# First self-attention of a two-layer decoder: the causal mask of the maximum's scores, added by VectorE in PSUM in place of two TensorE products

## What is computed

```python
q3 = (x @ wq).reshape(b, t, h, 3).transpose(0, 2, 1, 3)
k3 = (x @ wk).reshape(b, t, h, 3).transpose(0, 2, 1, 3)
v = (x @ wv).reshape(b, t, h, hd).transpose(0, 2, 1, 3)
dot_scores = jnp.einsum('bhtd,bhsd->bhts', q3, k3) * scale
geo_bias = q_on_dir[..., :, None] * k_on_dir[..., None, :]
scores = jnp.where(causal, dot_scores + geo_bias, -jnp.inf)
attn = jax.nn.softmax(scores, axis=-1)
out = jnp.einsum('bhts,bhsd->bhtd', attn, v)
```

## Time and profile before

| | us |
|---|---|
| median of 3 runs | 1267.47 |
| lowest and highest | 1267.25, 1268.99 |
| the profiled execution, its own time | 1272.5 |
| span of that execution, first to last instruction | 1270.6 |
| TensorE matmul busy over the span | 1150.3 (91%) |
| VectorE busy | 719.7 (57%) |
| ScalarE busy | 565.0 (44%) |
| GpSimd busy | 105.4 (8%) |
| mean granted TensorE clock | 0.956 of full speed |

### The profile page before, as it was taken

The page is one execution under the profiler, slowest core; times in us unless marked ns, Lnnn a source line. Parts: engine busy times, 40 slices in busy tenths (PEclk is TensorE's granted clock), DMA queues, the critical chain, the costliest instruction groups (busy, mean ns, idle before and its releaser), DMA issues.

```text
span 1270.6 us, 19991 instructions
## 1 busy us (share of the span) xinstructions
PE 1150.3 (91%) x7418; PEld 720.2 (57%) x7418; DVE 719.7 (57%) x1054; ACT 565.0 (44%) x1084; POOL 105.4 (8%) x147
## 2 busy tenths in 40 slices
PE   4999999898988988869988999999999999998797
PEld 2453443442222322247866777877787887786465
DVE  4344445667888789661426466465646666673213
ACT  1344344154545555751214566456635564562210
POOL 0112232112100000010001000010001000100100
PEclk7799899898979999979999999999999999999799
DMA  7012212320000000000023233123634964400000
GB/s 205 14 51 100 89 37 100 115 76 1 1 1 1 1 1 1 1 18 1 1 67 112 62 91 74 34 52 83 150 85 100 214 144 101 101 18 1 1 17 17
DMA packets 56962, 74.20 MB, mean 58 GB/s; under 512 B 12443, under 2 KB 33446, under 8 KB 56870
## 3 DMA queue, kind: packets, MB, share of 16 engines
q1 hardware_dynamic: 53110, 69.26, 21.4%
q10 hardware_dynamic: 3760, 3.67, 0.9%
HBM read 36.20 MB, written 15.73 MB: 41 GB/s over the span
## 4 chain that ended last, share of the span: by engine, by line
PE 79%; DVE 9%; issue 5%; ACT 4%; DMA 1%; POOL 1%; SPq 1%; ACTq 0%; POOLq 0%; DVEq 0%
PE p_unit L1665 20%; PE p_ring L1665 12%; PE p_out L1789 9%; PE p_ring L1685 8%; PE p_ring L1766 8%; PE p_ring L1732 7%; PE p_out L1755 6%; DVE halves L1454 2%; PE p_unit L1857 2%; PE p_ring L1710 1%; ACT prob_b L1238 1%; DVE prob_a L1468 1%; DVE x L1560 1%; PE p_ring L1724 1%; PE p_ring L1703 1%
## 5 line engine op out<-in xcount | busy, mean ns | idle before, releaser
L1454 DVE TENSOR_REDUCE halves<-p_ring 128x2 f32<-128x1024 f32 x128 | 156.2, 1220 | 65.8 <-PE p_ring L1710 65.6
L1252 ACT ACTIVATE prob_a<-p_ring 128x1024 f32<-128x1024 f32 x128 | 130.6, 1022 | 101.6 <-PE p_ring L1732 101.4
L1434 DVE TENSOR_REDUCE nmax<-p_ring 128x2 f32<-128x1024 f32 (+1 forms) x128 | 156.0, 1219 | 33.7 <-PE p_ring L1685 33.6
L1270 ACT ACTIVATE probT_b<-p_ring 128x512 f32<-128x512 f32 x144 | 84.5, 598 | 202.2 <-PE p_ring L1766 200.7
L1238 ACT ACTIVATE prob_b<-p_ring,nmax 128x512 f32<-128x512 f32 (+1 forms) x192 | 158.6, 837 | 18.3 <-DVE nmax L1434 18.0
L1685 PE MATMUL p_ring<-stacks 128*128 128x512 f32 x512 | 151.4, 418 | 8.9 <-ACT prob_b L1238 5.3
L1487 DVE COPY probT_b<-p_ring 128x512 f32<-128x512 f32 x112 | 77.1, 688 | 133.5 <-PE p_ring L1766 133.0
L1766 PE MATMUL p_ring<-ident,prob_b 128*128 128x128 f32 x1024 | 134.5, 274 | 0.3 <-ACT probT_b L1270 0.3
L1766 PEld LDWEIGHTS p_ring<-ident,prob_b 128*128 128x128 f32 x1024 | 116.2, 141 | 23.5 <-issue 14.8
L1732 PE MATMUL p_ring<-x_q,x_kq 32*128 32x512 f32 x512 | 124.4, 658 | 2.9 <-DVE halves L1454 2.9
L1454 DVE TENSOR_REDUCE wide_max<-p_ring 128x2 f32<-128x256 f32 (+3 forms) x64 | 52.6, 823 | 90.3 <-PE p_ring L1703 90.3
(11 more groups left out here) (226 smaller groups left out, 1614.1 us busy)
## 6 DMA issues: line engine op xcount, KB each, us to landing
stacks<-x_kd SPq DMA_DIRECT2D x64, 256.0 KB, 5.9
stacks<-splitH_b SPq DMA_DIRECT2D x80, 128.0 KB, 2.3
stacks<-splitL_b SPq DMA_DIRECT2D x80, 128.0 KB, 2.4
x_kd<-early SPq DMA_DIRECT2D x19, 256.0 KB, 2.0
x_v<-x_vd SPq DMA_DIRECT2D x8, 512.0 KB, 4.1
x_kd<-xT SPq DMA_DIRECT2D x13, 256.0 KB, 2.0
x_vd<-early SPq DMA_DIRECT2D x11, 256.0 KB, 2.0
a_st<-a_image SPq DMA_DIRECT2D x64, 32.0 KB, 1.8
```

The source lines that it names most:

```text
L1252: nc.scalar.activation(prob_place(key), slot_of("S2", key), ACT.Exp, accum_out=x0_sums[:, m:m + 1]).then_inc(done["E2"], 1)
L1270: keep_turned(act, key, lambda o, i: nc.scalar.activation(o, i, ACT.Copy)).then_inc(done["VA"], 1)
L1434: nc.vector.tensor_reduce(nmax[:, n % 4, 0:heads], src, AX.X, ALU.max, negate=True).then_inc(done["M"], 1)
L1454: nc.vector.tensor_reduce(to, src, AX.X, ALU.max, negate=True).then_inc(done["M1"], 1)
```

## The change

The mask leaves TensorE. `identb` is gone, and `hidden` is now the same triangle in fp32, in the same 512 bytes a partition that the two took. `S1` is the two score products alone. Before each reduction of `A0`, `M1` adds the triangle to the last 128 keys of both heads in one instruction on VectorE (128 partitions x 256 elements), read from PSUM and written back in place, and is linked, so that the reduction waits for its end. At the program's start GpSimd has one memset and one select less. The order of all other steps is as before.

```diff
-        identb = put("identb", [128, 128], BF16)
-        hidden = put("hidden", [128, 128], BF16)
+        hidden = put("hidden", [128, 128])
...
             nc.gpsimd.memset(ident[:, :], 0.0)
-            nc.gpsimd.memset(identb[:, :], 0.0)
             nc.gpsimd.memset(hidden[:, :], 0.0)
...
-            for t in (ident, identb):
-                nc.gpsimd.affine_select(out=t[:, :], in_=t[:, :], compare_op=ALU.not_equal, fill=1.0, base=0,
-                                        pattern=[[-1, 128]], channel_multiplier=1)
+            nc.gpsimd.affine_select(out=ident[:, :], in_=ident[:, :], compare_op=ALU.not_equal, fill=1.0, base=0,
+                                    pattern=[[-1, 128]], channel_multiplier=1)
...
                         src = slot_of("S1", key)[:, :, 0:w]
+                        dve.wait_ge(consts_ready, 1)
+                        last = src[:, :, w - 128:w]
+                        link(nc.vector.tensor_tensor(last, last, hidden[:, :].unsqueeze(1).to_broadcast([128, 2, 128]),
+                                                     ALU.add))
...
                         for aa in range(2):
                             r = 64 * pr + 32 * aa
-                            nc.tensor.matmul(o[:, aa, 0:w], a0_st[r:r + 17, G % HELD, 1, 128 * i:128 * i + 128],
-                                             a0_st[r:r + 17, G % HELD, 0, 0:w], start=True, stop=False,
-                                             tile_position=(r, 0))
-                        for aa in range(2):
-                            ins = nc.tensor.matmul(o[:, aa, w - 128:w], identb[:, :], hidden[:, :], start=False, stop=True)
+                            ins = nc.tensor.matmul(o[:, aa, 0:w], a0_st[r:r + 17, G % HELD, 1, 128 * i:128 * i + 128],
+                                                         a0_st[r:r + 17, G % HELD, 0, 0:w], start=True, stop=True,
+                                                   tile_position=(r, 0))
```

## The result

| | before | changed |
|---|---|---|
| median of 22 runs each, taken side by side | 1269.20 us | 1275.47 us |
| lowest to highest | 1265.58 to 1271.82 | 1266.18 to 1282.15 |
| ratio, 95% interval | | 1.0048 [1.0032, 1.0063] |
| profiled execution, own time | 1272.50 | 1271.99 |
| its span | 1270.6 | 1270.1 |

The change costs about 6.3 us. The forecast was 1.8 us less, 1265.7 with a range up to 1271.5; the median lies 4 us above the top of it. The runs of the changed kernel spread over 16 us, those of before over 6.

A forecast was written before the change was run, and what follows sets the result against it. TensorE sets the pace from 31 to 195 us, busy 153.5 of 164.0. Terms -3.9 + 1.25 + 0.65 + 0.27 = -1.7, taken as -1.8 with 0.1 for the first tick: 1267.5 - 1.8 = 1265.7 us, range 1262.3 to 1271.5.

The forecast's parts named there:

- Value-product ticks: Ticks where a value product follows the mask at once and TensorE decides: 17 save 0.22 us each, 3.9 in all.
- ticks without one: About 30 ticks with nothing between mask and unit: the unit waits for ScalarE to empty `p_unit`, so nothing is saved.
- the two behind L1438: Two ticks following `mt`: the next unit waits 1.19 us for VectorE's `a_q` anyway, so nothing is saved.
- `dt` ticks: Six ticks whose unit waits for VectorE's emptying of `dt` behind a reduction; five lose 0.25 us each, 1.25 together.
- The seventh group's: Its `dt` emptying, with VectorE busy when scores come: whole add 0.45 counts, plus 0.20 at the layer norm: 0.65 us lost.
- the first `mt` tick: VectorE is still with a wide reduction when `mt` is to be emptied; the next unit waits: about 0.27 us lost.
- rival B: TensorE's clock falls more often behind `dt` waits, 2.7 us each: one fall 1268.4 (chance 0.15), two or more from 1271.1 (0.15).
- four kept the clock: Argument against more clock falls: of six `dt` ticks in the profile before, two had a fall and four did not.
- the other rule that the prediction weighed, the one on semaphores: Skill's claim that a semaphore after each VectorE operation costs nothing extra: losses 0.12 smaller each, time 1264.9; not followed.
- C: VectorE's add takes 0.69 us, so `dt` and `mt` ticks lose more: net +1.0 us, 1268.5; chance 0.07.
- D: Ticks shift and one of TensorE's present clock falls goes away: -4.5 us, 1263.0; chance 0.15.
- E: All 64 mask pairs on TensorE count, 0.22 us each: 14.1 us saved, 1253.4; chance 0.03.

The follow-up runs named there:

- The rerun: Both kernels unaltered, run and profiled again beside the kernel before: changed kernel 1276.61 us (ratio 1.0070), kernel before 1269.36 us (1.0012).

## Why the prediction was wrong

**The terms of the sum were nearly right.** I set the start of each score pair of the two profiles beside each other, in ticks where both had the same clock. Value-product ticks got shorter by 0.22 (one by 0.16), ticks without one did not change, nor did the two behind L1438. The `dt` ticks got longer by 0.29 to 0.37 where 0.25 was put down: the add starts 0.08 after the scores in place of 0.05, and L1435 took 0.78 for 0.70. The seventh group's grew by 0.53 (0.65), the first `mt` tick by 0.14 (0.27). With the eighth `dt` tick, which lies in a fall, put at 0.3 and the first tick of all at -0.2, these steps add up to about -1.6 us; the forecast had -1.8. The add's price, 0.429, and its link, 0.04 between add and reduction, were right; the idle time ahead of `normed` came to 1.36 in the tick of the earlier trace rows, where "about 1.2" stood.

**The step that failed is the one that left TensorE's clock as it was.** The forecast's sum has no term for the clock; it stood only in rival B. "TensorE's clock falls more often" had the right mechanism, the right place and nearly the right idle time, but was given 0.30 in all, and "four kept the clock" was read from a single execution. The rerun shows that the kernel before changes from one execution to the next: two falls behind `dt` ticks in one, none in the other. The two falls of the first profile were a sample, not the kernel's state. The changed kernel had four, 17.1 us at half clock, in both of its profiles. What decides is how often each of the six ticks falls, so that counting "one more fall" or "two" was the wrong frame.

**Its size was off in both factors.** A fall was priced at 2.7 us, from one that lasted 6.8 us; the two profiles of the kernel before put such a one at 3.0, and one of 3.4 us costs 1.6, as the fourth group's tick shows (0.87 in the value product, 0.74 in the unit), and 1.4 net of what the tick gained. Against that, the number is larger. The share of the span at half clock is twice what the mean clock lacks to 1: 2 x 0.0445 x 1270 = 113 us in the changed kernel, 2 x 0.037 x 1268 = 94 before. Those 19 us more, if all of them cost as much as in this stage, 1.6 / 3.4 = 0.47 us each, are 9 us; less the 1.8 of the steps, about +7. Over the 35 runs of the kernel before, the time falls by some 600 to 670 us per unit of clock, which gives 0.0075 x 640 = 4.8, and +3. The measured +6.3 lies between; the mean clocks do not fix it better.

**The rule of the skill.** The falls stand behind waits of under 1.5 us of TensorE, amid small products. The Trainium skill ("TensorE: Matmul & The Clock Gate", section "Why this matters for your kernels") would have let such waits pass; here they are where the time went. I noted the contradiction in the prediction and still counted the rule against B when weighing it. The link's price (0.04 us after the add's end, where L1435 starts 0.09 before its forerunner's) bears the rows out against the other rule that the prediction weighed, the one on semaphores, as well.

**The other rivals.** C falls: no add took over 0.433. D falls: the fall at 149 us came again, though shorter (3.4 us), and two came on top. E falls: ticks without a value product did not move.

**What is shown and what is open.** Shown: the loss is time at half clock in this stage (5.8 us in the ticks with falls in the second pair of profiles, the other ticks 0.7 shorter). Filling the wait leaves no fall behind a `dt` tick in the profiles of four kernels, and brings the changed kernel back by some 8 us, with all its adds. A small pair in the same place does not. Open: how much of the 19 us lies in this stage in every run, since behind its `dt` ticks the first pair of profiles shows 7 us more, the second 17, and falls outside it vary between executions; and what makes a tick fall. The wait was not lengthened by itself with the work around it unchanged. Without any mask the ticks alone give some 5 us, and neither that run (1268.6) nor the filled one (1265.0) got them all; whether the lost products alone, with the wait as before, would have cost the clock is not shown. The clocks of 0.958 to 0.961 are too near each other to rank those kernels.

## What to carry to other kernels

Work taken from the engine that sets the pace counts only in the ticks which that engine ends; elsewhere it becomes idle time, and on TensorE idle time can lower the clock of the work behind it. Before moving small products off TensorE, look for waits of up to about 1.5 us that get longer amid small work, and fill them or keep the work there. Judge a clock by many executions: one profile of this kernel had two falls in a stretch where the next had none, and two profiles with the same mean clock had their falls in different places.

## What the hardware showed that I had not expected

- In the changed kernel the clock fell to its lower level behind waits of 0.76 us (fourth group) and 1.27 us (seventh), each amid small products, for 3.4 or 6.8 us; no other length was seen in the stretch. It stayed up behind 1.36 us in the fifth group, and without a mask it fell in the fourth behind 0.35.
- Products that add zeros, in six places, made the kernel before 0.2% faster (0.62 us in each) and took the changed one from 1275.5 to 1266.7 us (1.07 in each).
- A wait that only moves to another buffer (0.35 for `normed` and 0.61 for the slot, in place of 0.76) did not keep the clock up: it fell in the same tick, for 6.8 us in place of 3.4.
